# A two-layer convolution on one core: row means from the rounded input, the image's share of them moved into the first phase, the first convolution behind the mix, and one of two loads issued by ScalarE

## The reference

```
x = x + conv0(gn(x))      # quantised: q = round(clip(gn(x)/scale, -127, 127)), 3x3, int weights, * scale*w_scale + bias
x = x + irfft2(conv1(rfft2(gn(x))))   # complex 3x3 convolution of the spectrum, plus complex bias
```

## Time and profile before

| | |
|---|---|
| profiled execution | 3688.6 us |
| its span | 3686.8 us |
| TensorE busy | 2952.2 us (80%) |
| VectorE busy | 3147.2 us (85%) |
| ScalarE busy | 1888.0 us (51%) |
| GpSimd busy | 1481.3 us (40%) |
| TensorE row-mean matmuls, line 1031 | 512.8 us |
| VectorE rounding and clamping in the loop, lines 818 and 820 | 433 ns and 310 ns each |
| DMA, mean | 198 GB/s |

### The profile page before, as it was taken

How to read it: one execution, slowest core, us unless ns; L and a number is a source line. 1 busy time by engine, 2 the same in 40 slices (tenths; PEclk the granted TensorE clock), 3 DMA queues, 4 the chain that set the end, 5 groups by cost and what they waited for, 6 DMA issues and landing times.

```text
span 3686.8 us, 126585 instructions
## 1 busy us (share of the span) xinstructions
PE 2952.2 (80%) x45732; PEld 2630.6 (71%) x45732; DVE 3147.2 (85%) x5880; ACT 1888.0 (51%) x2799; POOL 1481.3 (40%) x1984
## 2 busy tenths in 40 slices
PE   0000004899999999999999999999999999999998
PEld 0000002688888888888888888888888888888888
DVE  8999995688888888888888888888888888888886
ACT  8999991344444444444444444444444444444443
POOL 4777100344444444434443333443443433344444
PEclk9999999999999999999999999999999999999999
DMA  8777760366666666666666666666666666666655
GB/s 312 239 239 239 239 216 13 100 205 197 201 199 203 202 200 200 204 197 200 201 202 195 197 194 193 202 197 197 204 199 196 204 194 192 201 193 206 199 181 180
DMA packets 630696, 730.98 MB, mean 198 GB/s; under 512 B 76752, under 2 KB 602160, under 8 KB 614736
## 3 DMA queue, kind: packets, MB, share of 16 engines
q1 hardware_dynamic: 482640, 588.71, 50.1%
q10 hardware_dynamic: 147456, 134.28, 12.7%
HBM read 262.58 MB, written 134.22 MB: 108 GB/s over the span
## 4 chain that ended last, share of the span: by engine, by line
PE 54%; SPq 13%; DMA 11%; issue 11%; DVE 7%; ACTq 1%; ACT 1%; POOL 1%; DVEq 0%; POOLq 0%
PE y_ps L986 14%; PE mean_b L1031 9%; PE x_ps L973 7%; PE conv_ps L1018 7%; SPq L464 7%; PE fin_ps L1005 6%; DMA halo<-quant 4%; DMA out<-img 4%; PE t_ps L964 4%; SPq L386 3%; PE conv_ps L1020 2%; DVE scaled L763 2%; DMA img<-in_x 2%; PE fin_ps L1000 2%; DVE scaled L764 1%
## 5 line engine op out<-in xcount | busy, mean ns | idle before, releaser
L734 POOL TENSOR_SCALAR eo<-img,norm 128x256 f32<-128x256 f32 x512 | 477.9, 933 | 1458.5 <-PE t_ps L964 1248.9
L986 PEld LDWEIGHTS y_ps<-mix_w,stack 128*128 128x128 f16 x24576 | 793.5, 99 | 119.6 <-DMA stack<-xn 6.0
L986 PE MATMUL y_ps<-mix_w,stack 128*128 128x64 f16 x24576 | 809.3, 194 | 4.5 <-DMA stack<-xn 4.4
L562 ACT ACTIVATE y_hi<-y_ps 128x512 f16<-128x512 f32 x512 | 305.6, 597 | 889.3 <-PE y_ps L986 889.3
L548 ACT ACTIVATE xt<-t_ps 128x512 f32<-128x512 f32 x512 | 305.7, 597 | 629.2 <-PE t_ps L964 506.6
L973 PE MATMUL x_ps<-dft,xt 128*128 128x128 f32 x4096 | 541.6, 275 | 0.0
L839 DVE SCALAR_TENSOR_TENSOR img<-conv_ps,cst,img 128x512 f32<-128x512 f32 x512 | 383.1, 748 | 169.3 <-PE conv_ps L1020 153.1
L1031 PE MATMUL mean_b<-row_mean,img 128*128 128x48 f32 x4096 | 512.8, 273 | 8.4 <-DVE img L839 8.4
L1031 PEld LDWEIGHTS mean_b<-row_mean,img 128*128 128x128 f32 x4096 | 504.1, 196 | 18.2 <-DVE img L839 17.5
L826 DVE SCALAR_TENSOR_TENSOR xn<-x_ps,norm,xn 128x512 f16<-128x512 f32 x512 | 383.7, 750 | 140.7 <-ACT xn L555 120.0
L973 PEld LDWEIGHTS x_ps<-dft,xt 128*128 128x128 f32 x4096 | 498.3, 192 | 0.0
(11 more groups left out here) (134 smaller groups left out, 5111.6 us busy)
## 6 DMA issues: line engine op xcount, KB each, us to landing
stack<-xn SPq DMA_DIRECT2D x2048, 132.0 KB, 2.7
img<-in_x SPq DMA_DIRECT2D x1024, 128.0 KB, 2.9
out<-img ACTq DMA_DIRECT2D x1024, 128.0 KB, 3.0
img<-in_x SPq DMA_DIRECT2D x120, 1024.0 KB, 4.9
halo<-quant SPq DMA_DIRECT2D x192, 193.3 KB, 3.3
halo<-quant SPq DMA_DIRECT2D x64, 169.1 KB, 3.2
row_mean<-table_row_mean SPq DMA_DIRECT2D x1, 768.0 KB, 15.4
spread<-table_spread SPq DMA_DIRECT2D x1, 512.0 KB, 14.6
```

The lines of the kernel that those rows point to most:

```text
L734: nc.gpsimd.tensor_scalar(even, rows[:, :, 0:F], norm[v][:, 2:3], None, ALU.add).then_inc(shift_s, 1)
L986: last = nc.tensor.matmul(y_ps[t % 2][:, g, b, :], stack[:, t % 2, g, first:first + F], mix_w[:, 2 * at + b, g, f, part, :], start=i == 0, ...
```

## The change

Three things at once, with what they need:

1. Row means come from elsewhere. The mean of img after layer0 is the mean of x plus the mean of the convolution's result. The first is now taken in the first phase by TensorE (`image_means`, with a table as weights and the image moving) and kept in DRAM per sample (`kept`, 48 x 256), and read back at step 6 of the sample before (`load_means`). The second follows from sums over the rounded input: `row_means` now takes `rounded_w` as weights and `quant` as the moving operand, fp16, two matmuls of 258 columns per pair, right behind the pair's convolution. ScalarE copies the sums at step 9 (`rq`), and at step 12 `mean_rows` takes them through a 3x3 convolution of sums (`conv_a`), adds the kept ones and the shift, ten fp32 matmuls (twenty passes).
2. ScalarE writes the scaled pair as int16, which rounds it; VectorE's MAGIC operation goes, the clamp reads int16 and writes fp16. `quant`, `halo` and `conv0_w` are fp16 instead of bf16.
3. Order: on TensorE the mix comes before the convolution, the row mix of step 14 directly behind the transform; on VectorE rounding comes before layer0. ScalarE issues the load of the odd row block of a pair (`load_odd`), after its store of the same step.

```diff
-MEANS_OF = {14: (0, 1), 15: (2, 3), 0: (4, 5), **{t: (t + 5,) for t in range(1, 11)}}
...
-                for hb in (2 * j, 2 * j + 1):
-                    sp.dma_start(img[u][:, hb, :], src[:, :, hb, :]).then_inc(pair_s[u][j], 16)
+                sp.dma_start(img[u][:, 2 * j, :], src[:, :, 2 * j, :]).then_inc(pair_s[u][j], 16)
...
+            sp.dma_start(sums[1], table["sums_runs"]).then_inc(runs_s, 16)
...
+            for g in range(R):
+                sp.dma_start(raw_a[C * g:C * g + C].rearrange("p o a b -> p o (a b)"), flat0).then_inc(weight_s, 16)
+            sp.dma_start(scale_o, scale_weight[None, :].to_broadcast([P, C])).then_inc(weight_s, 16)
...
+            def keep(n, k, u):
+                sp.wait_ge(sums_s, n + 3)
+                sp.dma_start(kept[k], rmx[:, u, :]).then_inc(kept_s[u], 16)
+            def load_means(k, u):
+                if not (isinstance(k, int) and k == 0):
+                    sp.wait_ge(meanc_s, k)
+                sp.dma_start(rmx[:, u, :], kept[k]).then_inc(rmx_s[u], 16)
...
+                        sp.wait_ge(p1_pe, (2 * i + u - 2) * QU + q + 1)
...
+                act.wait_ge(p1_pe, QU * (n + 1))
+                act.wait_ge(kept_s[u], 16 * (i + 1))
+                nc.scalar.activation(rmx[:, u, :], sums_ps[u], ACT.Copy).then_inc(sums_s, 1)
...
-                act.wait_ge(rounded_s, PAIRS * k + j)
-                nc.scalar.activation(scaled[:], img[u][:, 2 * j:2 * j + 2, :], ACT.Identity,
+                act.wait_ge(quant_s, PAIRS * k + j)
+                nc.scalar.activation(whole, img[u][:, 2 * j:2 * j + 2, :], ACT.Identity,
...
+            def load_odd(k, u, j):
+                src = x[k].rearrange("c (h r) w -> c r h w", r=R)
+                act.dma_start(img[u][:, 2 * j + 1, :], src[:, :, 2 * j + 1, :]).then_inc(pair_s[u][j], 16)
...
+                    if conv and t == STATS_AT - 1:
+                        act.wait_ge(rq_s, PAIRS * (s + 3))
+                        nc.scalar.activation(rq[:], rq_ps, ACT.Identity, scale=q_scale).then_inc(rqe_s, 1)
...
+                    if mix and t >= 2 and ahead:
+                        act.wait_ge(store_s[(t - 2) % STORES], stored(s, t - 2))
+                        load_odd(s + 2, u, t - 2)
...
-                nc.vector.tensor_scalar(rows, scaled[:], MAGIC, MAGIC, ALU.add, ALU.subtract).then_inc(rounded_s, 1)
-                dve.wait_ge(rounded_s, PAIRS * k + j + 1)
-                nc.vector.tensor_scalar(rows, rows, CLIP, -CLIP, ALU.min, ALU.max).then_inc(quant_s, 1)
+                nc.vector.tensor_scalar(rows, whole, CLIP, -CLIP, ALU.min, ALU.max).then_inc(quant_s, 1)
...
+            def image_means(i, u, tab):
+                n = 2 * i + u
+                for q in range(QU):
+                    pe.wait_ge(load_s[u][q], loaded(i))
+                    if q == 0:
+                        pe.wait_ge(sums_s, n + 1)
+                    for hb in range(QB * q, QB * q + QB):
+                        last = nc.tensor.matmul(sums_ps[u], tab[:, 48 * hb:48 * hb + 48], img[u][:, hb, :],
+                                                start=hb == 0, stop=hb == HB - 1)
+                    last.then_inc(p1_pe, 1)
...
-                pe.wait_ge(x1_s, done(k, c))
+                pe.wait_ge(quant_s, PAIRS * k + c + 1)
...
                 for hb in (2 * c, 2 * c + 1):
-                    for half in range(2):
-                        nc.tensor.matmul(mean_ps[half], img[u][:, hb, F * half:F * half + F], row_mean[:, hb, :],
-                                         start=False, stop=False)
+                    last = nc.tensor.matmul(rq_ps, rounded_w[:, hb, :], quant[:, hb, :], start=hb == 0, stop=hb == HB - 1)
...
+            def mean_rows(k, i, u):
+                pe.wait_ge(rmx_s[u], 16 * (i + 1))
+                pe.wait_ge(rqe_s, k + 2)
                 pe.wait_ge(zb_s, k + 1)
                 for half in range(2):
+                    for dw in range(3):
+                        nc.tensor.matmul(mean_ps[half], rq[:, F * half + dw:F * half + dw + F], conv_a[:, dw, :],
+                                         start=dw == 0, stop=False)
+                    nc.tensor.matmul(mean_ps[half], rmx[:, u, F * half:F * half + F], ident[0:48, 0:48], start=False, stop=False)
                     last = nc.tensor.matmul(mean_ps[half], norm[u][:, 2:3].to_broadcast([P, P]), channel[:],
...
+                    if conv and t == IMAGE_AT + 2:
+                        mix_rows(s + 1)
+                    if runs(mix, conv, t + 1):
+                        mix_pair(s, t + 1)
                     if conv and t == STATS_AT:
                         group_stat(s + 1, meane_s, 0, gmean_s)
                     d, c = conv_of(t)
                     if conv if d == 1 else ahead:
                         conv_pair(s + d, c)
-                    if conv and t == IMAGE_AT + 2:
-                        mix_rows(s + 1)
-                    if runs(mix, conv, t + 1):
-                        mix_pair(s, t + 1)
+                        for m in range(c) if d == 2 and c == 1 else ():
+                            row_means(s + d, m)
+                        if d == 1 or c:
+                            row_means(s + d, c)
```

More of the change, by code:

```diff
@@ L85, in shape_tables @@
             for r in range(R):
-                rm[:, r, b, j, :] = eye * wave[j, R * b + r] / N
-    tab["row_mean"] = rm.reshape(P, HB, 3 * C)
+                rm[0, :, r, b, j, :] = eye * wave[j, R * b + r] / N
+                rm[1, :, r, b, j, :] = eye * wave[j, HB * r + b] / N
+    tab["sums"], tab["sums_runs"] = rm.reshape(2, P, HB * 3 * C)
+    rw = np.zeros((P, HB, P), np.float16)
+    hi, lo = halves(RSCALE * N * rm[0].reshape(P, HB, 3 * C))
+    rw[:, :, 0:48], rw[:, :, 48:96] = hi, lo
+    for c in range(C):
+        rw[R * c, 0, 96 + c] = 1.0
+        rw[R * c + R - 1, HB - 1, 112 + c] = 1.0
+    tab["rounded_w"] = rw
+    ca = np.zeros((8, C, 3, 3))
+    for dh in range(3):
+        co, si = np.cos(th * (dh - 1)), np.sin(th * (dh - 1))
+        turn = np.array([[1, 0, 0], [0, co, si], [0, -si, co]])
+        for part in range(2):
+            ca[3 * part:3 * part + 3, :, :, dh] = (turn.T / (RSCALE * N))[:, None, :]
+    ca[6, :, :, 2] = -wave[:, N - 1] / N
+    ca[7, :, :, 0] = -wave[:, 0] / N
+    tab["coef_a"] = ca.reshape(P, 9)
     tab["channel"] = np.concatenate([np.repeat(eye, R, 0), np.zeros((P, 2 * C))], 1) / (2 * R)
@@ L169, in build @@
     table = {k: nc.inline_tensor(v, name=f"table_{k}").ap() for k, v in shape_tables().items()}
+    kept = nc.dram_tensor("kept", (samples, 48, N), fp32, kind="Internal").ap()
     ctx = ExitStack()
@@ L235, in build @@
         quant_f, halo_f = flat(quant[:]), flat(halo[:])
+        whole = flat(scaled[:]).bitcast(mybir.dt.int16)[:, 0:2 * N].rearrange("p (a w) -> p a w", a=2)
         stack_f = flat(stack[:]).bitcast(fp32)
@@ L242, in build @@
         raw0h = stack_f[0:96, 720:864].rearrange("p (o a b) -> p o a b", o=C, a=3)
+        raw_a = stack_f[:, 1056:1200].rearrange("p (o a b) -> p o a b", o=C, a=3)
+        scale_o = stack_f[:, 1200:1216]
+        coef_a = stack_f[:, 1216:1225]
+        term_a = stack_f[:, 1232:1280].rearrange("p (b o) -> p b o", b=3)
+        halo_w = halo_f.bitcast(fp32)
+        sums = [halo_w[:, HW // 2 + 1536 * i:HW // 2 + 1536 * (i + 1)] for i in range(2)]
         taps_d = stack_f[:, 864:1056].rearrange("p (t m o b) -> p t m o b", t=2, m=2, o=C)
@@ L490, in _ @@
                     sp.sem_inc(tick_s, 1)
+                    sp.wait_ge(p1_pe, (samples - 2 + u) * QU + q + 1)
+                    sp.sem_inc(tick_s, 1)
+                keep(samples - 2 + u, u, u)
+            for u in range(2):
+                sp.wait_ge(kept_s[u], 16 * (SP2 + 1))
+                sp.sem_inc(tick_s, 1)
             for b in range(STORES):
@@ L926, in period @@
                         iy_low(s + 1)
+                    if conv if t < PAIRS - AHEAD else ahead:
+                        d, jq = quant_of(t)
+                        round_pair(s + d, jq, isinstance(i, int) and s + d == 0)
                     d, c = conv_of(t)
@@ L931, in period @@
                         stats_var(s + 1)
-                    if conv if t < PAIRS - AHEAD else ahead:
-                        d, jq = quant_of(t)
-                        round_pair(s + d, jq, isinstance(i, int) and s + d == 0)
                     if mix:
```

106 lines of the change are left out of this document (72 added, 34 removed).

## The result

The changed kernel takes 3503.9 us, the median of four runs (3492.8 to 3526.1), beside 3691.9 us (3686.2 to 3700.1) for four runs of the kernel before: a ratio of 0.949, 95% interval 0.945 to 0.953. The profiled execution took 3507.2 us, its span is 3505.4, so 181.4 us less than the span before.

The account below looks back on a forecast made before the run. VectorE was taken to bound the first phase, TensorE the main loop. From 3688.6: loop -236, before the loop -17, late start +10, ScalarE's copy +5, giving 3451 us; range 3370 to 3590.

Parts of the forecast that it names:

- The main term: Loop, TensorE: fp16 row means take 0.22 instead of 0.83, plain step 5.33 to 4.72 us, 9.8 us less per sample.
- the likeliest branch: Whole kernel: the likeliest outcome, 3451 us with its own range 3390 to 3510, chance 56%.
- VectorE's need: Loop, VectorE: needs 5.13 us a step with the old rounding, 4.54 with the new, just under TensorE's 4.72.
- rival 3: Loop, VectorE: slow int16 clamp at 0.75 us, need 4.99, +0.27 per step, +134 us, 3585 us; chance 8%.
- theory A: Follow-up forecasts, VectorE needing 5.13 us a step: without row means about 3470 us, with old rounding about 3670.
- The added wait: Step 10, TensorE: second statistics matmul no longer covered by the mix, its wait grows by 1.4 us per sample.
- That cover: ScalarE's odd load: the store it waits for is issued a whole step ahead, so the wait costs nothing.
- the upper bound of 1.8: Loop, convolution's halo waits: the new order takes back 1.5 of some 1.8 us per sample, between 0 and 1.8.
- Before the loop: First sample's convolutions, between first phase and loop: row means of 1.75 us go, -17 us in all, between -28 and 0.
- Rival 1: First phase: image sums at TensorE's 1.2 GHz take 28 us an image, +334 us, 3775 us in all; chance 15%.
- Rival 2: Loop, issuing queues: ScalarE's three issues take 0.85 us each, cycle 4.88, +0.16 per step, 3530 us; chance 12%.
- Rival 4: Loop's irregular steps: gain turns into waits, 3 us more per sample, about 3545 to 3640 us; chance 9%.

## Why the prediction came out as it did

**The main term was right, for an incomplete reason.** The plain step went from 5.33 to 4.72 us, by the old 0.83 and the new 0.22. But the prediction put the whole gain on TensorE. It gave the new order 1.5 us a sample and charged it 2.2 in new waits, a net cost of 0.7, and it gave ScalarE's load nothing. Undone in the changed kernel the two cost 80 and 148 us; put into the kernel before, the load gives 17; and without its row-mean matmuls the kernel before gains 106 of 412. Much of this meets in one place, SyncE's queue and the transfers that wait in it; statistics waits and the clock behind waits have their part. The prediction said that two loads and four restacks "would nearly fill a 4.72 step", and then did not say what happens if they do. That the sum still came within 53 us is in part luck: the time lies in the likeliest branch's own 3390 to 3510, but the loop gave 79 us less than forecast, and 24 us of unforeseen gain ahead of it covered a third of that.

**A step that was wrong and moved nothing: VectorE's need.** "VectorE now needs 5.33 less the wait of 0.20, 5.13" and "without it VectorE would be the bound at 5.13" are wrong: with the old rounding VectorE runs a step in 4.73, and a plain step of 4.50 with the same rounding stands in the trace of the kernel without row means. It was the distance of a whole step less the one wait that its row names, in a step set by TensorE, and such distances hold slack that no row names: from the clamp's start to the next operation's are 0.44 us in the earlier trace rows and 0.21 where VectorE is pressed (2047.53 to 2047.74 in the run with the old rounding). The same error is in the 4.54 for the new kernel. It cost nothing in the sum, since there both numbers were used only to say what is hidden (rival 3's 4.99 stands on them too); theory A of the runs without row means and with the old rounding rested on it, and fell in both.

**The loop's 2.5 us per sample** (7.6 predicted, 5.1 found), term by term from the step table, each against what its step was to be by the prediction's terms:

- Step 12, +0.8. The passes of `mean_rows` take 0.133 each and not the 0.104 of the row means, 0.6 of it. Whether that comes from weights that change after each pass was not tried.
- Steps 10 and 11, +0.9. The added wait was put at 1.4, and it is 2.08 instead of 0.68 in the rows shown. What was not in the sum is the low clock behind it. The small operations put first gave back 3.4 us a sample: this wait was the dearest thing left, and cheap to avoid.
- Steps 1 and 2, +1.4. The load "waits for the store of the pair before; that store is issued a whole step ahead, so I price the wait at nothing". That cover failed on SyncE. The prediction looked at what is queued behind this wait on ScalarE, and not at the restack behind the same wait on SyncE. With the restack ahead, 1.2 us came back.
- Steps 3, 4 and 6 to 9, +0.5 in small waits.
- Steps 5 and 13, -0.4: the halo wait went entirely, as the upper bound of 1.8 had it.
- Steps 14 and 15, -0.8 (step 0 adds 0.05): the row mix of step 14 waits some 0.3 and not 0.8 (0.27 in the rows of one sample); the rest is not traced to a cause.

**Before the loop, -36 instead of -17.** The means of 1.75 us went as priced. What was not foreseen is that TensorE then rose to 2.4 GHz at 619 us; in the kernel before it stayed at 1.2 up to the loop's first steps (the turn at 682.59 takes 1.11 us, the one at 685.86 0.60). Its convolution there now waits for VectorE, and a step takes 1.96 us.

**The first phase, +10.3.** The late start was priced at 10 and came to 10.29 (57.62 - 47.33). Its parts were not as priced: SyncE begins the row of eight weight loads 5.1 us later than before (31.91 instead of 26.82), where the tables were put at 4, and the nine new small loads take some 4.6, where they were put at 6. The 5 us for ScalarE's copy did not come. VectorE is back to back to the end.

**The range.** Its lower end, 3370, does not follow from the bounds named for it: they take 25, 9 and 11 us off 3451, which is 3406. Nothing hung on it.

**The rivals.** Rival 1, image sums at 1.2 GHz, did not happen: 0.218 a pass, and 15.67 us for the images that begin slow, far from 28. The Trainium skill ("TensorE: Matmul & The Clock Gate", section "Why this matters for your kernels") advises keeping the engine busy to get to full rate, and here the trace agrees. It does not explain the stretch ahead of the loop, though: TensorE was busy 17.16 of 18 us there before and stayed low, and after is busy 12.02 of 18 and rises. Rival 2, the queues, did not bind ScalarE, which of a thousand us still waits 297.4 for TensorE's transposes and 35.2 for its mix (161.8 and 292.9 before), but SyncE's queue was the near bound. Rival 3 did not happen: the int16 clamp takes 0.30. Rival 4, gain turned into waits, is what happened in part: 79 us in the loop, where it was given 94 to 190.

## What to carry to other kernels

When a step gets shorter, add up again what each issuing engine has to issue in it, and ask what stands behind its waits. Here one load moved off SyncE was worth 17 us with long steps and 148 with short ones. Before moving a large operation past a small chain between two engines, put the chain's small operations first in the queue of the engine that does them: 0.6 us of them held up 2.1 us of TensorE and then its clock. The distance from start to start on an engine that waits is no measure of what it needs. Nor is the sum of its durations, since operations overlap: the ten of VectorE's step in the run with the old rounding add up to 5.23 us and fit in 4.73. Look at a stretch with shorter steps, or one where the engine is the one waited for.

## What was unexpected of the hardware

- TensorE's clock. In the changed kernel a wait of 2.08 us at step 10 with short matmuls around it was followed by passes at 1.2 GHz in step 11 (transform 1.92 us, not 1.06), and without that wait they ran at 2.4 GHz. It happens once ahead of the loop too: a wait of 2.08 us at 651.49 for the same operation, and the next three convolution passes take 1.44 us, not 0.81. A wait alone does not tell: the one before it, 2.28 us long and ended at 647.91, was followed by matmuls at full rate. Ahead of the loop, fp32 row means with 48 columns alternating with convolutions never raised the clock; with fp16 row means of 258 columns in their place the fourth convolution ran at 2.4 GHz. The run without row means has neither kind, and its convolutions there stay at 1.44 us up to the loop, with TensorE busy 10.86 of the 18 us. So leaving out the fp32 row means does not by itself raise the clock; what in the new work raised it was not tried alone.
- The granted clock of a window can miss this: before, 612 to 630 us shows 1.00, while three passes of 512 columns took 1.48 us in it and not 0.81. The first clock record in that trace begins at 696.6 us; the 1.00 ahead of it is no measurement.

```profile
617.14 1.48 PE L1018 MATMUL conv_ps<-quant,conv_w 128*128 128x512 bf16 x3
```

- Longer waits came with a lower clock. Without row means the kernel before runs its loop at a granted clock of 0.95 and not 0.99, and loses 2.3 us a sample more to slow passes.
- Issuing four restacks takes SyncE 2.54 us in most steps, and 3.10 or 4.33 in others; why is open.
- ScalarE writes int16 in 807 ns, as it wrote fp32 in 0.80, and VectorE reads 512 int16 in 0.30 us where 512 fp32 took 0.41.
